# Another merge order of four walks on each engine in a twelve-block decoder

## The chip, the cores and the metric

The kernel runs on one core of a Trainium2 chip. The metric is device time in microseconds (us), from one launch of the whole program; lower is better.

## What is computed

The reference takes `x` of 8 sequences x 256 positions x 128 features, and a context of the same shape, through twelve blocks: four layers of self attention, cross attention and feed-forward. Each block adds to `x` what it computes from the layer norm of `x`:

```python
x = x + _L0_attn_ref(_layernorm(x, axis=-1), ...)     # distance scores, exp, softmax
x = x + _L0_xattn_ref(_layernorm(x, axis=-1), ctx, mask, ...)  # 16 heads, squared relu
x = x + _L0_ffn_ref(_layernorm(x, axis=-1), ...)      # three dense layers of signs
x = x + _L1_attn_ref(...)                             # 16 heads, relative bias
x = x + _L1_xattn_ref(..., ctx, ctx, mask, ...)       # 16 heads, shifted positions
x = x + _L1_ffn_ref(...)                              # 8 experts of rank 16, top 2
x = x + _L2_attn_ref(...)
x = x + _L2_xattn_ref(ctx, ctx, ..., mask, ...)
x = x + _L2_ffn_ref(...)                              # 8 experts, routed
x = x + _L3_attn_ref(...)                             # rotary, window, grouped heads
x = x + _L3_xattn_ref(..., ctx, ctx, mask, ...)
x = x + _L3_ffn_ref(...)                              # 8 experts, top 2
```

A block of one sequence needs the former block of that sequence only, except for the routed experts of L2_ffn and L3_ffn, which gather rows of several sequences.

## The kernel before

The eight sequences are split over two streams: stream 0 takes sequences 0, 2, 4, 6 and stream 1 takes 1, 3, 5, 7, and each has four PSUM banks and its own tiles in SBUF. In each block a stream works through its four sequences (items), one behind the other. All of `x` stays in SBUF.

Every one of the five engines (tensor, scalar, vector, gpsimd, sync for the DMA issues) has a program made of Python generators, which are run once, when the kernel is built; what they emit is a straight line of instructions. The generator of a block, such as `L1_ffn(s, b, j)`, yields between small pieces of work; a piece, here called a step, is some one to eight instructions, mostly with one wait for a semaphore ahead of them. `alternate` strings the blocks together into walks. An engine has four: walks 0 and 1 are the main work of stream 0 and of stream 1, walks 2 and 3 are what is done ahead for the next block's items (the norm, the q, k and v products, masks, routing) of stream 0 and of stream 1. Between the walks of one engine, and between the engines, semaphores keep data dependences; nothing else ties one walk to another.

The order in which an engine interleaves its four walks is written out in the table `TURNS`, one string for each engine. Turn `i` of the string belongs to walk `i % 4`, and its character, a digit in base 36, says how many steps that walk advances before the next turn. In "2003", walk 0 does two steps, then walk 3 does three. Each engine executes its instructions in the order emitted. `Hand.wait_ge` drops a wait whose value the engine has already waited for.

The stages stand one behind the other, with the fronts of the next block mixed in: roughly, in the time before, L0_attn to 100 us, L0_xattn to 209, L0_ffn and L1_attn to 680, L1_xattn (whose scores are shifted through DRAM, tiles `skew`, `skew_room`) to 995, L1_ffn to 1152, L2_attn and L2_xattn to 1500, L2_ffn with its sorted experts to 1675, L3_attn to 1833, L3_xattn to 1937, and L3_ffn with sorted experts to the end. In the sorted experts, rows are gathered by indirect DMAs into blocks of one expert (`sorted`), pass the two products of that expert, whose weights SyncE loads for each block (`P<-in_L3f_rows`, `kz<-in_L3f_rows`), and are written back by GpSimd's indirect DMAs (`back<-mask,block_to`), from where SyncE reads them for each item (`kz<-back`). `stacks` is room in DRAM through which pieces of q and k are moved between partitions.

Lines that the trace names most: L746 is the helper of all matmuls, L1512 of ScalarE's activations, L1838 to L1849 of VectorE's operations, L2504 GpSimd's power of a norm, L2583 its indirect write, L2680 SyncE's `dma`. L358 is `Hand.wait_ge`.

Of the kernel before, what the change touches and what calls it, by code (L numbers as in the profile page):

```python
# [52 lines left out]
    "tensor": ("0100110012003211110011001300130021002100210021002100110011001300140062002100210022001500210031002100120021001200"  # L53
        "2300120040010011001001020010101100100201001101003100110010010010220011003100110011001100111011001100210033002200"
        "1100210011001300110011003100420041001110010021100200110020010100101011001100120020101300100112001001010021002101"
        "0200110012002300110012001100410010100100202011001100321021002300110021001001410030011001010011001001010011001200"
        "1200210041003100220012001100410012001100110021003100120034002100130011001100110041001100130014001100330013001300"
        "2100110021001200110033001200110011003100110012002100210011001100120021005400110011002100120023001200210021002100"
        "1200230012001200210031001100110011001200260031001200230041001200130011001200110011004200440032001200130011001100"
        "3200210012002100120022003100120023006100120024001100110011001200230041001200240011002200310012002200220032001200"  # L60
        "1400210031001100230023003200330032001100510012001200120011001100110012001100120043002300110011002200310011001100"
        "3300110022001200130011001100310011001100120021001200220031001200110012006100120024001200210012002300410012002400"
        "1100120011004200230010100120020101030010610021002300120011004300110041003200120021001100210011002100220012002100"
        "2300110022001200110011003100110011001100210012001100211010100100211011002100110020102200120020011100100101021100"
        "1400110023002100410012001100120011001200210022002100130012001200110021001100210031002100210011001100210011001100"
        "1100210012003200210022001100220011001100120011002100120021001210010010100110120011001100111001001300130012003101"
        "1100100112020300430021001100130011002100310011002100110011002100120011002400140012002100120011002100210021002200"
        "3100410012001200110021002100130011001100210011001300110011001100110021001010212012002010020021001100120011001100"
        "1100210013002200110210010200220101001100110011001100410031001100110021001100120011001100120012001200110012002100"
        "2300210022001100110041001100410011002100110021001100110021001100110011001200230022001100110011001200110012001200"  # L70
        "1100120011001100310023003100230011001100130022001200110031003200120012002100110011002200110022001100210022001300"
        "1100310031001200120013001100120021001100220012001100110011001200230021001100310022001100210012001100140041002200"
        "3100110011001200240011002200310011003100120012001200110021002100210021001100110011001300140011002100220021001210"
        "011001001410041002100210010021002100110020013001400161007002a301010011001200210012001200110023002300130011002100"
        "1100110021001200230021001100110011001200110011001100110011001100110011101100211001001200130012004100101001002100"
        "1100110015002700110021001100110101001200210012001100220021001100200111001200500132001100140011001300110011002100"
        "1100120032001100110011100100301011003300220011001010220023001100120023002601030112001100110011003200110021001001"
        "3200120041008200110014001200110013004200210011001300210011001010210030101100111011001100110011001110210011002500"
        "1100130013010201110112003101310011002100130032001300320021006100120014001100120013004100110013001100110011001100"
        "1100220011001010202001001100110021101200110013001200110021001100230014002100110011001100210013001200210012001001"  # L80
        "1100220010011001300102002100130043001300110012001100410011001100210011001100210011001100110031001100110031001010"
        "0100201010101100130022001510410022003200110022001101220011001100220011002200110010011100110010011100100112001200"
        "1200210032002100110011001100120011003100111021001100320010104100231011001100111001002100210021001200120012002100"
        "1200110021001100300102001100220011002100110011001200130012012001110021002100400111001100120012101210010012001100"
        "1310010031001100110021001100110032001200120012102110010011001100220022001010020031001101010011011100210011001001"
        "21002100110032002300202003002100101001001101120111010a100110051008011301040103003200j001610020016001910011001100"
        "41001200220011001100210011002300210041001200420018001600151004101e100f100110c1006100101041002002a00100104010p010"
        "01010201030013001200150012001500160100104100201031005100210021009100301103010500230013001c0014016100410041004100"
        "5001200141001100140011001200110013001300110011001100110112001300240012002100110012001100230033001e00150012001100"
        "2100101002001010010022100200120010200100111021003100110021101010021010100210021005001100310011004100110011010101"  # L90
        "2200100101003200210010012001030010013200310021001100100111001001410020018100200120013001510061002200110013001b00"
        "110017001a0016001x"),
    "scalar": ("0200110010111100210014002200210011004200220011001100210012001100330011002100110022001200310022001200110011001200"
        "1001001220110011002100100100110101001001110021001101201021001100120011001100100112100100501001003100101014001300"
        "2100210011004600110011001100110032001100110011002010510020011200110011002110521001001200110011001200210010101001"
        "0010330011001601110203002100120013001200210010102200110010104010410011003010410030100100110010013100510102001400"
        "1100100101001100200102001100210023010100120011004100110011002200130021006100110031002100110031002100110011001200"
        "2100330013001200120012002100120011001500260021002200210021001300310012001100110011001100230011002200110011002300"
        "1200210011003400120011001100120012002100120012003200120022001200110011002300120011002100220012001100220012003200"
        "1200110031001100120022002200230011003200110011003200110011001100120031001100120022001100120011001100220012003100"  # L100
        "1100120011002200210011001200120031001300410012001100230021001100220011001100110012001100110022001200420011001200"
        "2200220023001100320011001100320023002200210011002200120011002200110011002300110011001010010100100101001150103010"
        "1100130012010100100101003200210011001100410011003200120011001200210011001200110012003200110023005200110021003100"
        "1200220010100100110011001010140020100100140010011001100100102300101001001200510020010100110101002100110011002300"
        "2200240021002200210031002100310011001100220011001100110011001100110021002200110022001100120021001200120042001110"
        "0110251002001200130011001200120111011100101011102001020011001100210011003001010011002100110121001100120014001100"
        "1100210021002100110012001200220021002100110031001200220021001100110011001100140031003200120011004110130011200100"
# [2892 lines left out]
```

## Time and profile before

| | us |
|---|---|
| median of three runs | 2091.87 |
| lowest and highest run | 2087.24, 2092.49 |
| the profiled execution, its own time | 2096.31 |
| its span, first to last instruction | 2094.5 |
| TensorE busy | 1745.7 |
| VectorE busy | 1438.9 |
| ScalarE busy | 1035.9 |
| GpSimd busy | 461.7 |

The profiled execution is one of its own, beside the three runs. Its span leaves out 1.8 us around the first and the last instruction. The mean clock that TensorE was granted is 0.925 of full speed. Busy time of TensorE is that of its matmuls; its weight loads run beside them. Idle time before an instruction is listed with what released it.

### The profile page before, as it was taken

To read this page: it belongs to the slowest core of one execution; us is meant where nothing else is said; L and a number is where in the kernel's file an instruction comes from. 1 tells how busy PE (TensorE), PEld (TensorE's weight loads), DVE (VectorE), ACT (ScalarE), POOL (GpSimd) and SP (SyncE) were. 2 spreads that over 40 slices of the span, in tenths; PEclk is the share of its full clock that TensorE was granted. 3 is DMA by queue.
4 is the path that set the end of the run, shared out by engine and by line. 5 is a ranking of instruction groups with operands and counts; after the bars stand their busy time and mean duration, and the time that the engine had idled before them with its cause. 6 is when DMAs were issued, how large, how long until landed. Compare 5 with 4: busy or idle time off the path is not lost.

```text
span 2094.5 us, 39958 instructions
## 1 busy us (share of the span) xinstructions
PE 1745.7 (83%) x14536; PEld 1356.6 (65%) x14536; DVE 1438.9 (69%) x4894; ACT 1035.9 (49%) x2588; POOL 461.7 (22%) x448
## 2 busy tenths in 40 slices
PE   6588999999998677779998798899878867766885
PEld 5455687776776455546887576667658855654785
DVE  6689524777877579779888677767864456567643
ACT  3277525666765556656333354455434335631342
POOL 3300110000002000000546200000464544213442
PEclk9899999999999789989999899999989879976888
DMA  5334067000001988885201323323126543332356
GB/s 179 79 74 117 16 240 231 1 1 1 1 1 37 269 214 238 245 225 152 81 1 28 90 72 89 89 59 88 48 77 190 161 120 93 77 139 84 103 153 199
DMA packets 211051, 228.56 MB, mean 109 GB/s; under 512 B 16052, under 2 KB 179276, under 8 KB 210216
## 3 DMA queue, kind: packets, MB, share of 16 engines
q1 hardware_dynamic: 205864, 215.71, 36.3%
q0 software_dynamic: 4992, 10.30, 1.4%
q8 instruction: 116, 1.90, 0.4%
q14 instruction: 79, 0.65, 0.1%
HBM read 130.57 MB, written 94.98 MB: 108 GB/s over the span
## 4 chain that ended last, share of the span: by engine, by line
PE 49%; DVE 22%; DMA 11%; ACT 7%; issue 6%; POOL 2%; SPq 2%; another core or an unknown queue 0%; DVEq 0%; ACTq 0%; POOLq 0%
PE banks L746 42%; ACT P L1512 4%; PE banks L1061 3%; DMA stacks<-region 3%; SPq L2680 2%; DVE region L1918 2%; DMA back<-mask,block_to 2%; DVE P L1838 2%; DVE negm L1849 2%; DVE P L2090 1%; ACT region L1512 1%; DVE route L1838 1%; DVE region L2160 1%; DVE region L1838 1%; PE banks L1153 1%
## 5 line engine op out<-in xcount | busy, mean ns | idle before, releaser
L2504 POOL TENSOR_TENSOR norms<-norms,consts 128x2 f32<-128x2 f32 x112 | 81.6, 730 | 1224.2 <-DVE norms L1842 1223.8
L1512 ACT ACTIVATE P<-P,negm 128x256 f32<-128x256 f32 x512 | 240.8, 498 | 114.0 <-DVE negm L2110 64.7
L1512 ACT ACTIVATE P<-banks 128x512 f32<-128x512 f32 (+2 forms) x392 | 188.4, 511 | 164.9 <-PE banks L746 155.6
L1849 DVE TENSOR_REDUCE negm<-banks 128x2 f32<-128x512 f32 (+1 forms) x264 | 149.2, 591 | 34.9 <-PE banks L746 31.1
L1512 ACT ACTIVATE region<-banks 128x384 f32<-128x384 f32 (+4 forms) x221 | 108.5, 506 | 78.1 <-PE banks L746 55.4
L746 PE MATMUL banks<-kz,qs 128*128 128x256 bf16 (+1 forms) x512 | 122.5, 275 | 27.2 <-DMA kz<-stacks 9.9
L746 PE MATMUL banks<-bands,identb 128*128 128x160 bf16 (+1 forms) x768 | 142.4, 247 | 0.0
L746 PE MATMUL banks<-xnT,region 128*128 128x256 f32 x544 | 138.8, 389 | 3.2 <-ACT xnT L1512 3.1
L746 PE MATMUL banks<-region 64*128 64x256 f32 (+6 forms) x922 | 124.6, 356 | 9.9 <-ACT region L1512 4.1
L746 PE MATMUL banks<-qv,region 128*128 128x256 bf16 (+2 forms) x512 | 114.9, 266 | 18.6 <-ACT P L1512 15.4
L746 PE MATMUL banks<-qs,kz 128*128 128x256 bf16 (+2 forms) x512 | 112.1, 262 | 17.7 <-ACT P L1512 8.9
L746 PE MATMUL banks<-kz,region 128*128 128x256 f32 x512 | 121.9, 384 | 4.0 <-DVE skew_room L1838 2.8
L2583 POOL DMA_INDIRECT back<-mask,block_to x92 | 89.4, 972 | 120.7 <-DVE mask L2338 110.1
L746 PEld LDWEIGHTS banks<-xnT,region 128*128 128x128 f32 x544 | 99.4, 194 | 21.4 <-ACT xnT L1512 6.9
L746 PEld LDWEIGHTS banks<-kz,region 128*128 128x128 f32 x512 | 95.6, 191 | 19.9 <-DVE skew_room L1838 5.1
L1838 DVE TENSOR_TENSOR P<-P 128x512 f32<-128x512 f32 (+1 forms) x136 | 84.6, 663 | 30.2 <-ACT P L1512 29.2
L746 PEld LDWEIGHTS banks<-region 128*128 128x128 f32 (+3 forms) x922 | 79.9, 160 | 36.8 <-issue 14.9
L746 PE MATMUL banks<-P,region 128*32 128x256 f32 (+6 forms) x1408 | 93.3, 325 | 10.4 <-ACT P L1512 3.7
L2110 DVE CUSTOM_DVE_ANT_0 P<-banks,region 128x256 f32<-128x256 f32 x256 | 92.7, 420 | 9.4 <-PE banks L746 9.2
L746 PE MATMUL banks<-region,identb 128*128 128x256 bf16 x384 | 98.2, 284 | 0.0
L746 PE MATMUL banks<-region,qv 128*128 128x256 bf16 (+2 forms) x384 | 79.2, 269 | 22.6 <-DMA qv<-stacks 9.6
L1153 PE MATMUL banks<-perm,P 128*128 128x128 f32 x512 | 82.2, 290 | 18.6 <-ACT P L1512 9.2
(288 smaller groups left out, 4485.2 us busy)
## 6 DMA issues: line engine op xcount, KB each, us to landing
stacks<-region SPq DMA_DIRECT2D x178, 192.0 KB, 3.0
sorted<-qs SPq DMA_DIRECT2D x4, 4160.0 KB
skew<-region SPq DMA_DIRECT2D x64, 256.0 KB
qs<-stacks SPq DMA_DIRECT2D x24, 384.0 KB
kz<-stacks SPq DMA_DIRECT2D x48, 192.0 KB
skew<-region SPq DMA_DIRECT2D x64, 128.0 KB
skew_room<-skew SPq DMA_DIRECT2D x32, 256.0 KB
P<-skew SPq DMA_DIRECT2D x32, 256.0 KB
```

Source lines behind the costliest of these rows:

```text
L746: return p.e.matmul(o, lhsT, rhs, start=start, stop=stop)
L1061: i = p.e.transpose(s.T[:, k * S + t * 128:k * S + (t + 1) * 128], s.P[:, n // 2 % 2, n % 2, t, k * 128:(k + 1) * 128], ident)
L1153: m = p.e.transpose(s.T[:, k * S + t * 128:k * S + (t + 1) * 128], s.P[:, i % 2, 0, t, k * 128:(k + 1) * 128], ident)
L1512: return a.e.activation(o, i, f, **kw)
L1838: return v.e.tensor_tensor(o, a, b, op)
L1849: return v.e.tensor_reduce(o, a, AX, op, negate=negate)
L1918: step(v.e.tensor_copy(dst, t.unsqueeze(1).to_broadcast([128, dst.shape[1], S])))
L2090: m = v.e.tensor_tensor_reduce(Pq[:, t, :], bank[:, t * S:(t + 1) * S], addend(t), -1.0, 3.0e38, ALU.add, ALU.min, s.negm[:, t, i:i + 1])
L2110: m = v.e.tensor_tensor_reduce(Pq[:, t, :], s.bank[par][:, t * S:(t + 1) * S], rel[:, h, 128 - 128 * t:128 - 128 * t + S], -1.0, 3.0e38, A ...
L2504: g.e.tensor_tensor(room[:, :, 0], room[:, :, 0], pows[:, :], ALU.pow).then_inc(done, 1)
L2583: g.e.indirect_dma_start(s.back[:, :], to, s.block_y[:, n % 2, :], None).then_inc(s.stored[n % 2], 16)
L2680: d.e.dma_start(dst, src).then_inc(sem, 16)
```

## The change

All five strings of `TURNS` are replaced, nothing else. The order in which each engine merges its four walks differs in small places all along the kernel. It was found by a local search that starts from the former order. The strings are shorter (tensor 4386 to 3262 characters, scalar 3486 to 2230, vector 4070 to 2806, gpsimd 518 to 422, sync 1074 to 642), partly as fewer turns of zero steps stand between others. The steps they count are 3686 before and 3682 after for tensor, 3151 and 3147 for scalar, 3093 for vector, 412 and 406 for gpsimd, 865 for sync; what is missing are last steps behind which a walk had nothing left to do.

The core of the diff, the beginnings of the shorter two strings:

```diff
--- before.py
+++ after.py
@@ -50,130 +50,92 @@
 TURNS = {
...
-    "gpsimd": ("1100171001001001200120101001001160101001001100120021002100110011a01020101010021004010610010400110011001100110012"
-        "0021001100220010101070011101001001001210030011002100300111001001001002001010030011002100210010012101001001001400"
-        "1100210021003001012011002200110010102100130203010310010101110011001100110011004100210012002100120022300160013001"
...
-    "sync": ("2201020014001110101010014001201020011001201040101001100200320021001100220031001100210011002200340010040103110201"
-        "0010021210100100101021002011001012001001100101001001010010010010110030101101020011003300110021002100130031001200"
-        "1200210023001100110020100100111010104100120101010101021001101430100111003002001110013001110045002100320011002100"
...
+    "gpsimd": ("50022020101200110910100100120021002100116011103001010024001001010011801040010b1200110021001100220010101080020110"
+        "1510010012005001110010010010020011100200110021002100200111101001040012001100310031010010011003100403001080010011"
+        "0011001100110011004008010021001200210012002250014001200131002100320031001410010011100210030074100313002200220012"
...
+    "sync": ("3020200231010010080010020022e01100210011001100220011003100430022002401110020080200221010030050010030400325001011"
+        "0100230055015500201033003200230032100320200102010301101060310010500327002101010055005410530102003300220033002210"
+        "3010051035010312603100105004090042010300201034005500530022001200230050100300322008010010900200305001070040020201"
...
```

## Rows read from the trace of the kernel before

**Rows 1.** The page's part 1: the span, busy time of each engine, instructions.
```profile
span 2094.5 us, 39958 instructions
...
PE 1745.7 (83%) x14536; PEld 1356.6 (65%) x14536; DVE 1438.9 (69%) x4894; ACT 1035.9 (49%) x2588; POOL 461.7 (22%) x448
```

**Rows 2.** The page's part 4: the chain's time by engine.
```profile
PE 49%; DVE 22%; DMA 11%; ACT 7%; issue 6%; POOL 2%; SPq 2%; another core or an unknown queue 0%; DVEq 0%; ACTq 0%; POOLq 0%
```

**Rows 3.** Windows: length, busy PE, PEld, DVE, ACT, POOL; granted clock, DMA share, GB/s.
```profile
0.00:209.00 209.00, 154.14 (x1216) 112.63 (x1216) 160.48 (x385) 109.57 (x203) 42.97 (x47) 0.93 0.40 112
209.00:680.00 471.00, 448.92 (x3043) 336.69 (x3042) 309.85 (x1152) 272.27 (x765) 30.67 (x33) 0.99 0.18 59
680.00:733.00 53.00, 31.63 (x247) 21.08 (x248) 29.09 (x112) 28.95 (x68) 1.36 (x2) 0.72 0.93 270
733.00:995.00 262.00, 210.73 (x1769) 149.28 (x1768) 212.66 (x745) 166.44 (x386) 10.86 (x15) 0.92 0.78 215
995.00:1152.00 157.00, 145.99 (x785) 125.64 (x784) 134.25 (x395) 52.02 (x117) 91.06 (x116) 0.98 0.11 37
1152.00:1833.00 681.00, 568.55 (x6110) 448.98 (x6109) 446.35 (x1460) 324.30 (x779) 192.99 (x137) 0.93 0.36 96
1833.00:1937.00 104.00, 66.76 (x471) 50.51 (x468) 71.56 (x310) 25.80 (x76) 28.98 (x34) 0.69 0.33 112
1937.00:2095.00 158.00, 119.01 (x910) 111.76 (x908) 74.71 (x341) 56.57 (x200) 62.81 (x66) 0.86 0.50 151
```

**Rows 4.** Timeline from 697 us: start, length, instruction, [idle before it].
```profile
699.74 0.89 SPq L2680 DMA_DIRECT2D skew_room<-skew  x2
700.68 0.98 SPq L2680 DMA_DIRECT2D P<-skew  x2
...
703.34 0.40 PE L746 MATMUL banks<-kz,qs 128*128 128x256 bf16 x1 [9.30 <-DMA kz<-stacks]
...
703.53 0.42 PE L746 MATMUL banks<-region,identb 128*128 128x256 bf16 x1
```

**Rows 5.** Timeline of PE at 710 us.
```profile
710.61 0.27 PE L746 MATMUL banks<-region,identb 128*128 128x256 bf16 x1
```

**Rows 6.** Timeline of PE, the first and last of the 100 steps.
```profile
106.41 1.92 PE L746 MATMUL banks<-xnT,region 128*128 128x256 f32 x4
...
2035.84 1.06 PE L746 MATMUL banks<-kz,OTp 128*128 128x128 f32 x8
2036.73 0.50 PE L746 MATMUL banks<-region,OTp 128*128 128x128 f32 x3
```

**Rows 7.** Timeline of PE in L2_ffn.
```profile
1623.67 1.06 PE L746 MATMUL banks<-region,P 128*128 128x128 f32 x8
...
1625.56 1.14 PE L746 MATMUL banks<-region 128*128 128x128 f32 x8
...
1627.88 1.06 PE L746 MATMUL banks<-region,OTp 128*128 128x128 f32 x8
```

**Rows 8.** Timeline of DVE in L1_ffn.
```profile
1020.03 1.41 DVE L1846 SCALAR_TENSOR_TENSOR kz<-banks,OTp 128x256 f32<-128x256 f32 x4
...
1022.07 0.42 DVE L1838 TENSOR_TENSOR P<-skew_room 128x256 f32<-128x256 f32 x1
```

**Rows 9.** Timeline of POOL, DVE and PE from 1986 us.
```profile
1987.96 0.96 POOL L2583 DMA_INDIRECT back<-mask,block_to  x1 [0.30 <-issue]
1988.95 0.72 POOL L2504 TENSOR_TENSOR norms<-norms,consts 128x2 f32<-128x2 f32 x1
1989.70 0.17 DVE L1890 COPY kz<-region 128x2 f32<-128x2 f32 x1 [2.90 <-issue]
...
1990.44 0.69 PE L1298 MATMUL banks<-perm,kz 128*128 128x128 f32 x2 [1.17 <-issue]
```

**Rows 10.** The chain at the end: start, length, what; the first and last landing.
```profile
2046.00 7.26 DMA back<-mask,block_to
...
2084.29 4.21 DMA kz<-back
```

More of the change, by code:

```diff
@@ L52 @@
 TURNS = {
[L53 to L92, printed above, removed]
@@ new lines @@
+    "scalar": ("0300320013004210230020013100110013003200230041001400420023003100140042002001001200110201004101003001100103003101"
+        "2010350053010210301060102900520055001500310043008310310023016110021032002500301020113500260010030500360040103300"
+        "3200701001100100501060100300200182010100150102003001030042003001060053005500320061005300730014007500250026004500"
+        "2500250041004300540012002200340022002200340022004600220022002400220012003200120022001200220012002300320021001300"
+        "3400110032001200120053002200120033001100320022003200130032002100110022003200130022002200120011003100230021001100"
+        "1100230012003100130041001300330032002200110012002200110011002200120042002300220022002300210022002200320023002200"
+        "2100110024001100320011001100230011001110010300205100101020102502020062001300410042003100140033001300420033001400"
+        "7100430011001300310010102300211024100400200220100300300100100200420030012201220043001400330012003200520043004300"
+        "1100340074004400440023003100132029002500231101002001202002003400400102003001220020011300490042004400440041004400"
+        "4300210024004400330011005300301014200100240022002200240101002201301002004010520122002200300103013400430014004200"
+        "4500720054004600450051003400120025002100240049003200840012002200430054002700210014001100120022003100530022003600"
+        "2100120011001100110063002300330011003200110012001200761004006010010032200110011007310013100121013200310020016001"
+        "2001b001810022001200310023005c1017001710061003001010301081001300500104002100210011006200200150013100220013010200"
+        "11002501020062001100160012001210031009003021001029004101b10080010200200181002200130105003b0027100300861003003021"
+        "001028014100a0020100310062002001a300150014003b008500110011100820030010205200310013005400200102006101510131002300"
+        "500103001501020035001800291003009010e020020029003010a00181011001020021001601040028119g00101001102100120030100100"
+        "301024005600j001610105100101030057010200110046011c00111023009201g1002100170080103001060011100e001f01060080019300"
+        "2100110011001100381001001210050021300320d1002100g00260303020010090028001l00101001101061005003010020010101m002011"
+        "3010a30160013200d1010101021001003a001010030010100m00f00230018001320182003d00220023001100150020010300180203009x00"
+        "660020100700202002006010220020300a1066010200100112001001260010010200120010014001320142011100150012001h"),
```

138 lines of the change are left out of this document (60 added, 78 removed).

## The prediction

> **What bounds the kernel now.** I read the page first. TensorE (PE) is busy for 1745.7 of 2094.5 us, the next engine, VectorE (DVE), for 1438.9 [rows 1]. That leaves PE 2094.5 - 1745.7 = 348.8 us without work, one sixth (16.7%) of the span. The chain that ended last lies on PE for 49% of the span, on DVE for 22%, on DMA for 11% and on ACT for 7% [rows 2]: PE sets the pace for long stretches, and between them the chain hops over DVE, ACT and transfers.
>
> Where these stretches lie is in the windows [rows 3]. From 209 to 680 us PE is busy for 448.92 of 471 us: no order of the work can gain much there. From 680 to 733 us it is busy for only 31.63 of 53, with the DMA engines at 93%; from 733 to 995 us for 210.73 of 262; from 1152 to 1833 us for 568.55 of 681; in the last 262 us for 66.76 + 119.01 = 185.77. An order can gain in these. It can lose most easily where two engines are full at once: from 995 to 1152 us (L1_ffn) PE has 145.99 and DVE 134.25 of 157 us.
>
> The last column but two is the granted clock of PE. It is 0.72, 0.69 and 0.86 in the stretches where PE waits most. The same product of 128x256 bf16 takes 0.42 us at 703.53, right after 9.30 us of idleness, and 0.27 us at 710.61 [rows 4, 5]; the former is at 1.2 GHz, the latter at 2.4 GHz. PE busy time times (1 - clock), summed over the eight stretches, is 10.8 + 4.5 + 8.9 + 16.9 + 2.9 + 39.8 + 20.7 + 16.7 = about 121 us: what the low clock costs today.
>
> **The change, part by part.** Only strings of digits differ. Every instruction, tile, transfer and semaphore stays, and so does the order inside each of the four walks of an engine; what differs is which walk goes first where two meet. I laid the old order and the new one over the timeline, step by step (a step is what a generator does between two yields), and for each step took its start and the moment its last input was there.
>
> Of the 2746 steps with work on PE, 452 change places; on ACT 385 of 1771, on DVE 452 of 1989, on POOL 61 of 330, on SP 134 of 493. None goes further than some 15 places. Counted in pairs, 288, 248, 335, 34 and 96 pairs of steps change sides, 1001 in all. The strings also lose a few last turns that no walk needed; they issue nothing, so they cost nothing.
>
> What can be gained: a step on the chain that stood ready behind others, and now goes ahead of them, starts earlier by at most the smaller of its own slack and the work it passes. On PE that is 46.1 us in 100 steps, of which the first is one of the two that share the row at 106.41 and the last that at 2036.73, ahead of the one at 2035.84 [rows 6]. On DVE it is 26.6 us in 43 steps, on ACT 5.7 in 14, on SP 4.6 in 6, on POOL 0.9 in 1: together 83.9 us. Three places as samples:
> - On PE an expert product of stream 1 at 1627.88 goes ahead of three steps of stream 0 that began at 1624.6: 2.06 us earlier [rows 7].
> - On DVE the softmax multiply at 1022.07, whose inputs were there at 1018.6, goes ahead of the four scaled sums of 1.41 us at 1020.03 and what follows them: 2.04 us [rows 8].
> - On POOL the norm at 1988.95, ready at 1986.4, goes ahead of the indirect write at 1987.96. DVE stood idle for 2.90 us until 1989.70 and PE for 1.17 us until 1990.44 behind it [rows 9]; about 1 us of this should really vanish.
>
> What can be lost the same way: on PE 58 of the 227 steps that are moved ahead had inputs which, at the times of before, came too late for the new place. At most they add 24.4 us of waiting. The largest is the expert product of stream 1 at 1625.56 (ready at 1625.49), put ahead of three steps from 1623.67 on, 1.82 us [rows 7]. And a step of the chain that is passed by others starts later by what passes it, so long as nothing fills that again; the bound of this is 71.7 us on PE, 63.8 on DVE, 11.6 on ACT, 13.9 on SP and 0.7 on POOL, 161.7 in all.
>
> On SP the same. Just before PE's 9.30 us of idleness, stream 1's `skew_room<-skew` (0.89 us at 699.74, ready since 672.8) goes behind stream 0's `P<-skew` (700.68) and the `skew<-region` after it: 0.99 and 1.5 us for stream 0 against 3.8 us for stream 1, which had slack [rows 4]. At the end, stream 1's weight loads go ahead of stream 0's reads of `back`, and stream 0's last store goes behind stream 1's. At most 1.3 us, since the four waits for a landing that make most of the chain there, the first 7.26 us long and the last 4.21 [rows 10], are of transfers whose order in their own stream does not change.
>
> Two large moves that I cost at nothing: the `ctxT` load at 196.7 us goes behind steps that wait until 341 us, but PE reads it only at 666.5 us; three weight loads of L3_ffn at 1921.8 us go 8 us later, for products in the 1990s. Without that cover they would cost 8 us and more.
>
> **The sum.** An earlier step shortens the kernel only where the work that it releases is what PE lacks. Between nothing and all of the 83.9 us I take PE's idle share as the price, one sixth: -14.0 us. The PE waits by the same share: 24.4 x 0.167 = +4.1. The passed steps I take at nothing, since in each exchange the one that passes does work that had to be done anyway and the idle time after it takes up the delay. Net -9.9 us. Against the profiled execution's own time, 2096.31 us, that is 2086.4. This execution lies 4.4 us above the median of the three runs (2091.87), so the forecast is 2082. Bounds: -83.9 if all of it counts, and +24.4 if nothing comes earlier and every wait on PE does.
>
> **A rule against the rows.** The rows at 703.53 and 710.61 show PE at half its clock behind an idle stretch [rows 4, 5]. The Trainium skill says, under TensorE: Matmul & The Clock Gate (Part 1, the HAM clock gate), that the default state is throttled and activity releases it: the trace agrees with that. It adds that for modelling "the ramp penalty is <1% of a typical kernel span". By that, less than 21 us would hang on the clock here, and the third rival below would be worth 2 us at most; the rows give 121 us, and I go by the rows.
>
> **Rivals.**
> - *Exchanges between equals* (2092). Two streams do the same on other batches: what one gains at a place the other loses. For it: the passed steps' 161.7 us stand against the 83.9; 471 us are full of PE work. Against it: the places where PE idles are unevenly spread, and most of the large moves let a step with waiting readers pass one with slack, like those in [rows 8, 9].
> - *DVE waits in order* (2103). This is the slower one. DVE takes 278 steps ahead of others, of which 181 had inputs that came too late for their new places; the bound of the waits is 102.8 us, of which 27.9 lie from 840 to 1260 us, around the stretch where DVE is busy for 134.25 of 157 us [rows 3]. Behind a waiting DVE instruction stand all four walks, and PE's evictions among them. If a fifth of that bound arrives, it is 20.6 us: 2096.3 - 14.0 + 4.1 + 20.6 - 4.4 = 2102.6. It turns the sign once more than a tenth (9.9 of 102.8) arrives. Against it: inputs come earlier too, as their makers were moved as well.
> - *The clock follows* (2070). If PE's idle stretches shrink, some of the 121 us of low clock goes too. A tenth of it on top of the forecast gives 2082 - 12. For it: clock and idleness go together in [rows 3]. Against it: moves of 1 to 2 us hardly break up a stretch of 9.30 us.
> - That the strings do nothing is excluded: 1001 pairs stand the other way.
>
> **How the numbers follow.** A change of 0.3% (6.3 us) is about what a measurement of this kernel can tell from no change. Forecast, -10 us with its own range of 2074 to 2086: 0.44. The clock follows: 0.11. Exchanges between equals, 2086 to 2098: 0.24. DVE waits, above 2098: 0.21. Faster is 0.44 + 0.11 = 0.55, same 0.24, slower 0.21. The range goes from 2064, past the clock's 2070 by half of what it adds, to 2104, just above the DVE rival; a tenth is left out on each side.
>
> **What the profile after would show.** Busy times of all engines the same to within a few us, except that PE's may fall with its clock. If I am right, PE's idle time falls from 349 to about 339 us, its idle 9.30 us before 703.34 becomes some 1 to 2 us shorter, the 1.17 us at 1990.44 vanish, and the windows from 733 to 995 and from 1152 to 1833 us give most of it, while 209 to 680 us keeps its length. If the DVE rival holds, DVE's idle time behind PE and ACT grows and the window of L1_ffn gets longer. If the clock follows, the windows now at 0.69 to 0.92 show higher ones. I am wrong if the exchanges that pay lie where PE has enough to do, or if a moved SP or POOL step holds back a transfer of some microseconds that no other work covers.

## The result, and the profile after

The kernel became slower: 2111.20 us median of six runs (2108.26 to 2116.21) against 2091.43 (2087.24 to 2092.97) for the kernel before on the same chip, a ratio of 1.0097 with a 95% interval of 1.0081 to 1.0113. That is about 20 us where 10 us less were forecast. The profiled execution took 2114.68 us, its span is 2112.9. Line numbers after the change are 38 lower: L708 is the former L746.

The page of the kernel after: the span, the engines' busy time, the chain by engine, which answer to [rows 1, 2].

```profile
span 2112.9 us, 39940 instructions
...
PE 1757.5 (83%) x14536; PEld 1359.6 (64%) x14536; DVE 1441.4 (68%) x4894; ACT 1035.8 (49%) x2588; POOL 460.2 (22%) x448
...
PE 50%; DVE 23%; DMA 10%; ACT 7%; issue 4%; POOL 3%; SPq 2%; another core or an unknown queue 1%; DVEq 0%; POOLq 0%; ACTq 0%
```

PE's time without work rose from 348.8 to 2112.9 - 1757.5 = 355.4 us, and its busy time by 11.8 us: nearly two thirds of the loss in the traces is PE being busy longer with the same work. The other engines are as busy as before, to within 2.5 us.

The windows of the kernel after, same columns as [rows 3], with edges set to the same steps of PE, to the nearest microsecond or two:

```profile
0.00:210.00 210.00, 155.40 (x1212) 113.11 (x1213) 160.62 (x384) 108.37 (x202) 42.94 (x47) 0.93 0.39 111
210.00:683.00 473.00, 449.99 (x3047) 336.89 (x3044) 309.49 (x1153) 273.24 (x766) 30.15 (x33) 0.99 0.18 59
683.00:735.00 52.00, 30.42 (x246) 20.60 (x247) 28.67 (x110) 29.01 (x68) 1.36 (x2) 0.72 0.96 275
735.00:1000.00 265.00, 213.96 (x1769) 151.68 (x1768) 214.06 (x747) 165.53 (x384) 10.51 (x15) 0.92 0.77 213
1000.00:1164.00 164.00, 147.31 (x786) 125.57 (x785) 138.27 (x397) 52.37 (x117) 89.91 (x117) 0.99 0.10 34
1164.00:1857.00 693.00, 579.98 (x6085) 455.21 (x6088) 443.90 (x1460) 324.30 (x777) 193.91 (x137) 0.91 0.35 95
1857.00:1959.00 102.00, 66.47 (x501) 51.26 (x495) 71.48 (x310) 26.72 (x78) 29.68 (x35) 0.72 0.32 109
1959.00:2113.00 154.00, 113.96 (x906) 105.30 (x905) 74.92 (x340) 56.25 (x199) 61.73 (x66) 0.91 0.52 159
```

L1_ffn, which was 157 us long, is 164: there PE's idle time grew by 5.7 us and its busy time by 1.3. The row from 1164 us on is 12 us longer, and here PE's busy time grew by 11.4 us, at a granted clock of 0.91 instead of 0.93. In the last row it fell by 5.1 us, at 0.91 instead of 0.86. Apart from these two rows, L1_ffn and that from 1164 us on, the lengths differ by 1 to 4 us.

The two traces hold the same steps in each walk, so each step has a start in both. How far apart the starts of the PE steps lie, and how this distance changes from one place to the next, says where time is lost. "Old" is the range of the same number, also against the trace before, in the 9 to 16 traces of experiments that had the old order in the stretch. Steps near an edge can stand in another order after the change, which makes such a number uncertain by some tenths, and at 1833 us by more than 1 us:

```
stretch of before    after - before   old order, other traces
   0 to   20 us          +1.25          -0.29 to +1.30
  20 to   46             -4.26          -1.69 to  0.00
  46 to   75             +4.69          -0.00 to +0.01
  75 to  209             -0.25          -2.35 to +0.07
 209 to  680             +1.54          -0.23 to +0.02
 680 to  995             +2.30          -2.12 to +5.95
 995 to 1150             +7.07          -0.60 to +0.24
1150 to 1500             +2.88          -0.71 to +4.11
1500 to 1675             +3.90          -6.27 to +0.86
1675 to 1790             +1.06          -3.73 to +1.42
1790 to 1833             +3.72          -0.53 to +0.93
1833 to 1937             -2.26          -0.47 to +2.23
1937 to the end          -3.27         -14.64 to -1.96
```

The column sums to +18.4 us, the difference of the spans. Some stretches with few transfers repeat to hundredths or tenths of a microsecond, those with many do not. What stands clear of the repeats is L1_ffn (+7.07), a pair in L0_attn that nearly cancels (-4.26, +4.69), L3_attn's end (+3.72), L2_ffn (+3.90 from 1500 to 1675 us) and L0_ffn with L1_attn (+1.54); clear on the other side is only L3_xattn (-2.26). L2_ffn has less behind it than its range says: of the two other traces with the new order there, e15 shows +2.1 and e3 -6.0 us.

The experiments ran on four chips in turn, and the last stretch goes by the chip: -13.8 to -14.6 us in e1 to e3, -6.7 to -9.0 in e5 to e8, -11.5 to -14.4 in e9 to e12, -2.0 to -4.4 in e13, e14 and e16 to e18, all with the old order there. So its wide range is mostly that of chips.

Two places where PE is busy longer, in the trace before and in the trace after (L2_ffn and L3_attn's end):

```profile
1500.00:1675.00 175.00, 142.55 (x1164) 121.20 (x1162) 97.58 (x450) 70.03 (x209) 100.10 (x82) 0.89 0.42 131
...
1790.00:1833.00 43.00, 34.20 (x460) 25.94 (x459) 24.96 (x92) 23.81 (x58) 9.64 (x6) 1.00 0.31 75
```

```profile
1515.00:1694.00 179.00, 147.15 (x1166) 125.52 (x1165) 97.19 (x450) 69.90 (x210) 99.79 (x82) 0.85 0.41 128
...
1810.00:1857.00 47.00, 36.45 (x436) 26.59 (x440) 25.35 (x95) 23.88 (x56) 9.83 (x6) 0.93 0.28 69
```

PE's busy time grew by 4.6 and 2.3 us in them and the clock fell from 0.89 to 0.85 and from 1.00 to 0.93. One trace of each kernel can't say whether the new order brings that about or where the low stretches happened to fall.

### The profile page after: what moved, and what is told of

Its sections match the earlier page's. It is cut to its first block, busy times and chain, and to the rows that moved or that the text cites. A ratio compares the mean times of both kernels' runs of the same rounds, so it can differ in the third digit from the quotient of the medians.

```text
span 2112.9 us, 39940 instructions
## 1 busy us (share of the span) xinstructions
PE 1757.5 (83%) x14536; PEld 1359.6 (64%) x14536; DVE 1441.4 (68%) x4894; ACT 1035.8 (49%) x2588; POOL 460.2 (22%) x448
## 4 chain that ended last, share of the span: by engine, by line
PE 50%; DVE 23%; DMA 10%; ACT 7%; issue 4%; POOL 3%; SPq 2%; another core or an unknown queue 1%; DVEq 0%; POOLq 0%; ACTq 0%
PE banks L708 43%; ACT P L1474 3%; PE banks L1023 3%; SPq L2642 2%; DVE P L1800 2%; DVE region L1880 2%; DMA skew<-region 2%; DVE negm L1811 2%; DMA stacks<-region 2%; DVE route L1800 1%; DVE skew_room L1800 1%; ACT region L1474 1%; DVE region L1800 1%; PE banks L874 1%; DMA back<-mask,block_to 1%
## 5 line engine op out<-in xcount | busy, mean ns | idle before, releaser
L708 PE MATMUL banks<-bands,identb 128*128 128x160 bf16 (+1 forms) x768 | 145.1, 249 | 0.0
L708 PE MATMUL banks<-kz,qs 128*128 128x256 bf16 (+1 forms) x512 | 121.8, 274 | 26.2 <-DMA kz<-stacks 11.1
L708 PE MATMUL banks<-xnT,region 128*128 128x256 f32 x544 | 139.9, 390 | 3.3 <-ACT xnT L1474 3.1
L708 PE MATMUL banks<-region 64*128 64x256 f32 (+6 forms) x922 | 125.3, 358 | 8.8 <-ACT region L1474 3.6
L708 PE MATMUL banks<-qv,region 128*128 128x256 bf16 (+2 forms) x512 | 116.4, 268 | 16.9 <-ACT P L1474 13.6
L708 PE MATMUL banks<-qs,kz 128*128 128x256 bf16 (+2 forms) x512 | 113.3, 265 | 18.2 <-ACT P L1474 9.6
L708 PE MATMUL banks<-kz,region 128*128 128x256 f32 x512 | 122.0, 385 | 7.2 <-DVE skew_room L1800 5.0
L708 PEld LDWEIGHTS banks<-xnT,region 128*128 128x128 f32 x544 | 99.0, 193 | 22.6 <-ACT xnT L1474 7.5
L708 PEld LDWEIGHTS banks<-kz,region 128*128 128x128 f32 x512 | 95.8, 191 | 24.9 <-DVE skew_room L1800 8.3
L708 PE MATMUL banks<-P,region 128*32 128x256 f32 (+6 forms) x1408 | 93.9, 331 | 11.9 <-ACT P L1474 6.7
L708 PEld LDWEIGHTS banks<-region 128*128 128x128 f32 (+3 forms) x922 | 80.4, 161 | 34.6 <-issue 13.7
L708 PE MATMUL banks<-region,qv 128*128 128x256 bf16 (+2 forms) x384 | 79.2, 266 | 24.7 <-ACT region L1474 11.7
L708 PE MATMUL banks<-region,identb 128*128 128x256 bf16 x384 | 98.3, 284 | 0.0
```

Of the source, the lines that this page charges most:

```text
L708: return p.e.matmul(o, lhsT, rhs, start=start, stop=stop)
```

## The experiments

All use the kernel before and change only strings of `TURNS`. The kernel before ran at 2075 to 2094 us beside them, by chip; ratios are to the runs on the same chip, and single traces are compared by stretches.

**One part of the kernel at a time.** A cut at a time t gives each walk the steps that began before t in the trace before.

```diff
-TURNS = old order
+TURNS = old order before t1, new order from t1 to t2, old order from t2 on
+# t1, t2 in us: e1 0, 995; e2 995, 1152; e3 1152, 1675; e4 1675, end
```

> The new order on all engines for the steps that began before 995 us in the old trace, the old order behind. Theory 1 (the loss is local: each stage loses by its own exchanges, and what it loses stays lost): the two traces of whole kernels stand 5.3 us apart at 995 us, so +5 us against before (2096). Theory 2 (the loss lies in one place, L1_ffn, where VectorE waits in order): within 2 us of before. Theory 3 (the loss comes from the clock, by chance of where the low stretches fall, not from the places): any size up to 10 us, not tied to the 5.3.

> The new order only for the steps between 995 and 1152 us (L1_ffn with the fronts done beside it), the old one before and behind. Theory 1: the distance between the two traces grows there from 5.3 to 12.4 us, so +7 us (2098). Theory 2: nearly the whole loss, +15 to +20 us. Theory 3: near nothing, since TensorE has its full clock there in both traces.

> The new order only between 1152 and 1675 us (L2_attn, L2_xattn, L2_ffn). Theory 1: the distance grows there from 12.4 to about 18 us, so +5 to +6 us (2097). Theory 2: within 2 us of before. Theory 3: more, as PE busy time grows there by 5 us of the 12 in all.

> The new order only from 1675 us to the end (L3_attn, L3_xattn, L3_ffn). Theory 1: the distance is about 18 us at 1675 and 19.6 near the end, with 24 between, so +1 to +2 us (2093). Theory 2: within 2 us of before. Theory 3: any size, as the clock is lowest here.

Measured: 1.0048 (1.0030 to 1.0066), 1.0048 (1.0032 to 1.0065), 1.0018 (1.0001 to 1.0036) and 1.0022 (1.0001 to 1.0044). The four sum to 1.36% where the whole change cost 0.97%. The loss is spread, against theory 2, and adds up within the intervals, for theory 1. L1_ffn is longer by 7.35 us in e2's trace, as by 7.07 in the trace after, at a granted clock of 0.98 before and 0.99 after ([rows 3] and the windows above); a loss there has nothing to do with the clock, against theory 3. Both e1 and e2 lost more in the medians than expected: 10 us where it was 5, and 11.5 where it was 7; e2's interval holds the 7, that of e1 (6.2 to 13.7 us) begins above its 5.

**L1_ffn by engine.** The new order between 995 and 1152 us on some engines alone.

```diff
-TURNS[engine] = old order
+TURNS[engine] = old order, new between 995 and 1152 us
+# engines: e5 vector; e6 tensor; e7 tensor, vector; e8 vector, scalar, gpsimd
```

> In L1_ffn (995 to 1152 us) VectorE alone in the new order, the other engines in the old one. Measured is the stretch between the PE steps that stood at 995 and at 1150 us, which was 7.1 and 7.4 us longer in the two traces with the new order on all engines, and changed by -0.6 to +0.2 us in those with the old one. Theory 1 (VectorE's order makes PE wait): +5 us or more. Theory 2 (PE's own order, steps put ahead of what feeds them): below +1.5 us. Theory 3 (only both together): below +1.5 us.

> In L1_ffn TensorE alone in the new order. Theory 1: below +1.5 us in the stretch. Theory 2: +5 us or more. Theory 3: below +1.5 us.

> In L1_ffn TensorE and VectorE in the new order, ScalarE and GpSimd in the old one. All three theories: about +7 us in the stretch; less than +5 us would say that ScalarE or GpSimd has a part.

> In L1_ffn VectorE, ScalarE and GpSimd in the new order, TensorE in the old one. Theory 1: +5 us or more, as with VectorE alone. Theory 2 and theory 3: below +1.5 us.

The stretch grew by 6.65, 3.48, 6.95 and 9.32 us. VectorE's order alone is enough for nearly the whole loss (theory 1). That TensorE's alone costs 3.48 none of the theories had; the two do not add, since 6.95 us is what both together cost, and e8, with VectorE's, ScalarE's and GpSimd's order new and TensorE's old, loses more than the whole change. Where PE then waits with VectorE's new order alone, by the waits of e5 in that stretch (total, times, longest; lines of that kernel are one lower):

```profile
PE banks L745 <- DVE pick_w L1837: 2.8, 3, 1.3
PE banks L745 <- DVE kz L1845: 2.5, 1, 2.5
...
PE banks L745 <- DVE skew_room L1837: 2.2, 3, 1.9
```

In the trace before, PE waited there once for `pick_w`, 0.6 us, never for VectorE's `kz`, and 2.8 us for `skew_room`. What is new is the waiting for the first two.

**Which of VectorE's 56 exchanged pairs.** First the 10 in which a routing step is passed: the copy of the router's logits (`route`) or the weights `pick_w`. e11 takes them out of e5, e12 has them alone. Then, alone, the 10 between steps of the two main walks that are no routing steps (e13), and the 36 in which a front's walk has a part (e14).

```diff
-TURNS["vector"] = old order
+TURNS["vector"] = old order, but of the 56 pairs that change sides in L1_ffn:
+# e11 all but the 10 with route or pick_w passed (45 of the other 46)
+# e12 these 10;  e13 10 between the main walks;  e14 36 with a front's step
```

> In L1_ffn VectorE in the new order, but the 10 of its 56 exchanges in which a routing step (the copy of the router's logits or the weights pick_w) is passed by another are undone; the other engines in the old order. VectorE's whole new order cost 6.65 us in the stretch from 995 to 1150 us. Theory 1 (the routing chain is what PE waits for): below +2.5 us. Theory 2 (the products of stream against stream and the norms of the fronts cost it): above +4.5 us.

> In L1_ffn the old order, with only those 10 exchanges on VectorE made. Theory 1: above +4 us in the stretch. Theory 2: below +2.5 us.

> In L1_ffn the old order, with only the 10 exchanges on VectorE made in which steps of the two streams' main walks pass each other (products of the gates, skew_room and P; no routing step). Theory 2a (these cost it): above +2.5 us in the stretch from 995 to 1150 us. Theory 2b (the fronts' walks cost it): below +1 us.

> In L1_ffn the old order, with only the 36 exchanges on VectorE made in which one of the two steps belongs to a front's walk (the norms and the scaled rows for the next block). Theory 2a: below +1 us. Theory 2b: above +2.5 us.

The stretch grew by 4.20, 1.49, 2.78 and -0.38 us. The routing pairs hold 1.5 to 2.5 of the 6.65 us: theory 1 fails in both runs, theory 2 holds in e12 and misses in e11 (4.20 where it said above 4.5). The 36 pairs of the fronts cost nothing alone. e13 is above the mark of theory 2a, but, as shown below, some 1.1 of its 2.78 us come from an exchange that the new order doesn't make; without it e13 lies between 2a and 2b. 1.49 + 2.78 - 0.38 = 3.9, so 2.8 us arise only when they come together.

Three places show how. In the first, VectorE before made `pick_w` first, and then a norm and a product `P` of the other stream:

```profile
1017.56 0.16 DVE L1842 TENSOR_SCALAR pick_w<-small 128x2 f32<-128x2 f32 x1
...
1018.41 0.35 DVE L1838 TENSOR_TENSOR norms<-norms 128x2 f32<-128x2 f32 x2
...
1018.87 0.42 DVE L1838 TENSOR_TENSOR P<-skew_room 128x256 f32<-128x256 f32 x1
```

After, the product and the norm go first, and `pick_w` comes last:

```profile
1024.07 0.41 DVE L1800 TENSOR_TENSOR P<-skew_room 128x256 f32<-128x256 f32 x1
1024.40 1.38 DVE L1800 TENSOR_TENSOR norms<-norms 128x2 f32<-128x2 f32 x2
...
1025.90 0.16 DVE L1804 TENSOR_SCALAR pick_w<-small 128x2 f32<-128x2 f32 x1
```

The norm's two small operations take 1.38 us between them, where they took 0.35. Each of them ends some 0.02 us after an operation that GpSimd does at the same time:

```profile
1024.24 0.84 POOL L2514 TENSOR_TENSOR kz<-P 128x256 f32<-128x256 f32 x1
1025.05 0.72 POOL L2510 TENSOR_TENSOR P<-P,OT 128x256 f32<-128x256 f32 x1
```

So about 1 us of the delay of `pick_w` is not the work that goes ahead of it but what GpSimd adds to that work. PE, which had no pause there before, stands idle for 1.17 us:

```profile
1024.21 1.13 PE L708 MATMUL banks<-kz,region 128*128 128x256 f32 x4 [0.18 <-DVE skew_room L1800]
1026.51 1.16 PE L708 MATMUL banks<-perm,pick_w 128*128 128x128 f32 x8 [1.17 <-DVE pick_w L1800]
```

The second is a sample that the prediction gave for a gain [rows 8]. The product `P` at 1022.07 and the step behind it go ahead of the four scaled sums `kz<-banks,OTp` of 1.41 us, which stood at 1020.03. In e13, VectorE's timeline is now

```profile
1019.27 0.16 DVE L1838 TENSOR_TENSOR norms<-norms 128x2 f32<-128x2 f32 x1 [0.68 <-POOL norms L2504]
1019.47 0.60 DVE L1843 TENSOR_SCALAR xn<-x,norms 128x128 f32<-128x128 f32 x2
1019.98 0.42 DVE L1838 TENSOR_TENSOR P<-skew_room 128x256 f32<-128x256 f32 x1
1020.50 0.69 DVE L1838 TENSOR_TENSOR skew_room<-banks,region 128x512 f32<-128x512 f32 x1
1021.11 1.41 DVE L1846 SCALAR_TENSOR_TENSOR kz<-banks,OTp 128x256 f32<-128x256 f32 x4
```

and PE's, which had run on without a pause,

```profile
1018.02 1.89 PE L746 MATMUL banks<-xnT,region 128*128 128x256 f32 x8
1021.91 1.35 PE L746 MATMUL banks<-kz,region 128*128 128x256 f32 x5 [2.00 <-DVE kz L1846]
```

PE waits 2.00 us, and it waits for the scaled sums. They read a PSUM bank, and PE's next product of that stream needs the bank empty. The step that was passed was the one that PE wanted; it was in time in the trace before. But not all of this belongs to the change: in e13 a front's norm and scaled rows (`norms`, `xn`) stand ahead of the sums too, with VectorE's wait of 0.68 us for GpSimd, and in the new order they do not (nor in the old). In e11, where the sums come before that norm, the pause at the same product is 0.88 us, and the distance jumps there by 1.15 us instead of 2.25. In e5 and in the trace after there is no such pause at all: PE comes there later, having stood for `pick_w`.

The third place is the largest jump of e5 in the stretch, 2.73 us at the step that stood at 1131.01. Before, VectorE made the scaled rows at 1126.19 (0.59 us), the scaled sums `kz<-banks,OTp` at 1128.38 and the residual sum `x<-x,banks` at 1129.71. In e5 the residual sum and the rows go ahead of the scaled sums. VectorE, then GpSimd, then PE:

```profile
1135.59 0.49 DVE L1837 TENSOR_TENSOR x<-x,banks 128x128 f32<-128x128 f32 x2 [1.24 <-PE banks L745]
1135.99 2.17 DVE L1842 TENSOR_SCALAR xn<-x,norms 128x128 f32<-128x128 f32 x2
1138.08 1.40 DVE L1845 SCALAR_TENSOR_TENSOR kz<-banks,OTp 128x256 f32<-128x256 f32 x4
```

```profile
1136.14 3.77 POOL L2601 CAST kz<-perm 128x2048 bf16<-128x2048 f32 x2 [3.62 <-DVE x L1837]
```

```profile
1138.88 1.13 PE L745 MATMUL banks<-kz,region 128*128 128x256 f32 x4 [2.46 <-DVE kz L1845]
```

The scaled sums stand behind a step that waits 1.24 us for PE, and behind the rows, which take 2.17 us instead of 0.59: the residual sum releases GpSimd's casts, and the rows last until the first of them has ended. The experiments take this apart. In e12 and e14 the sums still go first, and the distance doesn't jump. In e13 only the residual sum goes ahead, PE waits 0.38 us and the jump is 0.64. In e5 and e11 the rows do too, PE waits 2.46 us and the jump is 2.73 and 2.76. So 2.1 us that no part has by itself arise here. In the trace after, with TensorE's order new as well, this pause is 1.29 us.

**One step of GpSimd.** The pair at 20 to 75 us came from one step, a memset of 128x4096 bf16. In the trace before it ran at 32.98 for 3.51 us, and VectorE's `tensor_scalar` of 128x256 f32 from SBUF to SBUF, otherwise 0.28 us, lasted until it ended:

```profile
33.63 3.01 DVE L1842 TENSOR_SCALAR kz<-kz 128x256 f32<-128x256 f32 x1
```

After the change the memset runs at 48.98, and now the next item's `tensor_scalar` takes 3.49 us, with PE behind it:

```profile
48.98 3.52 POOL L2495 MEMSET region<- 128x4096 bf16 x1
49.15 3.49 DVE L1804 TENSOR_SCALAR kz<-kz 128x256 f32<-128x256 f32 x1
...
53.02 0.95 PE L708 MATMUL banks<-kz 128*128 128x256 f32 x2 [2.82 <-DVE kz L1808]
```

e9 has the old order with this one step in its new place, e10 with it behind the norm that stood at 39.20 in the trace before, where VectorE has nothing to do. The whole edit is one string:

```diff
-    "gpsimd": ("110017100100100120012010100100116010100100110012...
+    "gpsimd": ("110017100100100120012010100100110011001070010012...   # e9
+    "gpsimd": ("110017100100100120012010100100110010700100110012...   # e10
```

> The old order on every engine, but GpSimd's memset of 128x4096 bf16 (3.51 us at 32.98) is put where the new order has it, behind the norm at 51.35; nothing else moves. Theory A (VectorE's tensor_scalar from SBUF to SBUF can't start while GpSimd's memset runs): the one at 33.63, 3.01 us long, falls to 0.3 us, and PE steps come 3 to 4 us earlier at 50 us; in its new place, from about 48, the memset makes another one last over 2 us, and PE waits for it near 50 us, so that little or nothing is left at 75 us. Theory B (the norms that the memset was moved past are what helps and hurts): the long tensor_scalar stays with the norms, not with the memset. Either way within 2 us at 75 us.

> The old order on every engine, but the same memset behind the norm at 39.20, where VectorE then waits 5 us for PE. Theory A: no tensor_scalar over 1 us, no wait of PE at 35 and none at 50: the PE steps at 75 us come 3.5 to 4.5 us earlier, and the whole kernel is 0.2% faster. Theory B: no gain at 75 us.

e9 moved PE's steps by -4.27 us from 20 to 46 and by +4.71 us from 46 to 75, to 0.02 us what the whole change did there. The timeline of e9, GpSimd and then VectorE:

```profile
48.40 3.52 POOL L2533 MEMSET region<- 128x4096 bf16 x1
```

```profile
48.58 3.48 DVE L1842 TENSOR_SCALAR kz<-kz 128x256 f32<-128x256 f32 x1
```

e10 moved them by -4.28 and 0.00. In its timeline the memset runs from 36.85, after VectorE's `tensor_scalar`, which takes 0.28 us:

```profile
36.85 3.51 POOL L2533 MEMSET region<- 128x4096 bf16 x1
```

```profile
33.34 0.28 DVE L1842 TENSOR_SCALAR kz<-kz 128x256 f32<-128x256 f32 x1
```

Theory A holds. The whole kernel measured 0.9983 (0.9964 to 1.0002), 2076.32 us median against 2079.99: the size fits, and the interval just touches no change. The Trainium skill says this under SBUF — State Buffer (Who interferes with whom): VectorE and GpSimd share a pair of ports, an instruction such as `tensor_scalar` in a two-port mode and a GpSimd instruction can't hold it together, and the one that starts later "fully blocks". The trace agrees: 3.01 and 3.49 us for an operation of 0.28, each ending some 0.15 us after the memset.

**The clock takes part.** The stall holds PE for 2.38 us in the trace before and for 2.82 after, and the loss is 4.3 and 4.7. The windows of the kernel before (clock in the last column but two) show what comes after the stall, PE busy all the time at a mixture of 1.2 and 2.4 GHz:

```profile
33.00:37.00 4.00, 1.65 (x10) 1.30 (x10) 4.00 (x5) 1.33 (x4) 3.49 (x1) 1.00 0.88 284
37.00:41.00 4.00, 3.98 (x11) 3.21 (x12) 2.55 (x11) 0.00 (x0) 0.72 (x1) 0.59 0.97 307
```

The kernel after has the same behind its stall:

```profile
53.00:57.00 4.00, 3.98 (x11) 3.21 (x12) 2.08 (x7) 0.00 (x0) 0.00 (x0) 0.57 0.02 4
```

e10 in the whole stretch:

```profile
33.00:41.00 8.00, 7.54 (x43) 6.62 (x41) 3.98 (x18) 3.49 (x7) 4.18 (x2) 1.00 0.85 272
```

At a granted clock of 0.57 to 0.59, 4 us of PE work hold 4 x 0.41 to 4 x 0.43 = 1.6 to 1.7 us of loss, which is the rest. In e10 the clock stays at 1.00.

**Undoing the places found, and L3_xattn.** e15 is the whole new order, but with L1_ffn in the old order and the memset in its free place. e16 is the old order with the memset in its free place and the new order between 1833 and 1937 us.

```diff
-TURNS = new order
+TURNS = new order, old between 995 and 1152 us; memset behind the norm of 39.20   # e15
-TURNS = old order
+TURNS = old order, new between 1833 and 1937 us; memset behind the norm of 39.20  # e16
```

> The new order everywhere but in L1_ffn (995 to 1152 us, old), and GpSimd's memset in its free place behind the norm at 39.20. The whole new order was 20 us slower. If the losses are local and add up: 20 - 7.1 for L1_ffn - 4.7 for the memset's new place = +8 us (2088 where before has 2080). Rival (the stages lean on one another, so that a repair in one place is lost again behind it): +15 us or more.

> The old order, with GpSimd's memset in its free place and the new order on all engines between 1833 and 1937 us (L3_xattn). If that stretch gains by itself: -4.3 - 3.3 = -7.6 us (0.9963). Rival (it was only shorter as it gave back what the stretch before had lost): the memset's -4.3 us alone (0.998) or less.

e15 measured 1.0032 (1.0012 to 1.0053), or +6.7 us; the two repairs bring back 0.65 points of the 0.97, as the sum of places said. One of them is more than a repair: the memset's free place is worth 4.3 us that the kernel before doesn't have either, so what the other places lose together is 6.7 + 4.3 = 11 us. e16 measured 0.9980 (0.9962 to 0.9997), 2089.39 against 2092.72: faster than the kernel before by 3.3 us, about the memset's part. Nothing of L3_xattn's shorter stretch can be told from the runs. In e16's trace it is 1.1 us shorter, against 2.3 in the trace after and 3.1 in e4, where the stretch before it had lost 3.7 and 5.5 us; so part of the gain there is loss given back.

**L3_attn's end.**

```diff
-TURNS[engine] = old order
+TURNS[engine] = old order, new between 1790 and 1833 us   # e17 all, e18 vector
```

> The new order on all engines between 1790 and 1833 us only. If the loss arises there: +3.5 to +5 us in the stretch from 1790 to 1833 us, where traces with the old order differ by -0.5 to +0.9 us. If it was brought along from the stretch before: below +1.5 us.

> The new order on VectorE alone between 1790 and 1833 us. If VectorE's order makes it: +3 us or more. If it is TensorE's or ScalarE's order: below +1.5 us.

The stretch grew by 2.13 us in e17 and by -0.11 in e18. So VectorE's order alone is not it. Against 3.7 us in the trace after and 5.5 in e4, e17 has 2.1; its clock stays at 1.00 in the stretch, where it is 0.93 in the trace after and 0.86 in e4. Whether the rest needs the new order before 1790 or is the clock's, and which step it is, stays open.

## Why the prediction was wrong

- **The sign.** The forecast was -9.9 us, the measured change about +20. The step that failed is in the sum: "The passed steps I take at nothing". Their bound stood there, 161.7 us, twice that of the steps that come earlier (83.9). I dropped it with the argument that the step that passes does work that had to be done anyway and the idle time after it takes up the delay. VectorE's new order in L1_ffn alone made the stretch 6.65 us longer. Its largest jump, 2.73 us, is a passed step that PE needed next, and what went ahead of it was more than work to be done anyway: a wait of 1.24 us, and an operation of 2.17 us instead of 0.59 while GpSimd's cast ran.
- **The sample on VectorE** at 1022.07 was counted as a gain of 2.04 us. In e11 and e13 it belongs to a stop of PE, 0.88 and 2.00 us, the latter with a norm ahead as well. In the trace after PE has no pause there, but nothing is gained either. The slack of the step that goes ahead was read from the trace, the slack of the one passed was not.
- **The sample on PE** at 1627.88 came where forecast in the order, but the step went ahead only together with the one at 1625.56 of [rows 7]; from 1602 to 1632 us the distance grew by 0.72 us in the trace after and fell by 0.51 in e3. No gain can be seen.
- **The sample on GpSimd** was right in mechanism and wrong in size: "about 1 us of this should really vanish". The norm does go first and VectorE's pause falls from 2.90 to 1.64 us, but PE's is 1.07 instead of 1.17 [rows 9]. GpSimd's timeline and then PE's after the change:

```profile
2008.99 0.72 POOL L2466 TENSOR_TENSOR norms<-norms,consts 128x2 f32<-128x2 f32 x1
2009.91 1.03 POOL L2545 DMA_INDIRECT back<-mask,block_to  x1 [0.20 <-issue]
```

```profile
2010.48 0.44 PE L1260 MATMUL banks<-perm,kz 128*128 128x128 f32 x2 [1.07 <-issue]
```

- **The 9.30 us** before 703.34 [rows 4] were to become 1 to 2 us shorter by SP's new order. They are 9.24:

```profile
707.21 0.40 PE L708 MATMUL banks<-kz,qs 128*128 128x256 bf16 x1 [9.24 <-DMA kz<-stacks]
```

- **The windows.** 733 to 995 and 1152 to 1833 us were to give most of a gain; they are 3 and 12 us longer. That 209 to 680 us keeps its length is right to 1.54 us.
- **The DVE rival** had the right sign, engine and stretch for the largest single part: VectorE's new order alone gives 6.65 us where the whole change gives 7.07 in L1_ffn. It had the mechanism in part. It spoke of VectorE waiting for late inputs, bound 27.9 us around that stretch, and such a wait, 1.24 us for PE, does stand ahead of the passed sums at the largest place. But with that wait alone PE lost only 0.38 us (e13). More comes from VectorE being busy with another step while PE waits, above all with one that GpSimd makes longer: the rows of 2.17 us there, the norm of 1.38 us ahead of `pick_w`. Its price, 20.6 us for the whole kernel, netted to +11 in its 2103; the loss outside L1_ffn was not shown to be VectorE's, and e18 says that at one place it is not VectorE's alone. It had 0.21 where the forecast had 0.44.
- **The exchanges between equals** would need the sum of the places to be zero. Of the places clear of the repeats, all but the first of the L0_attn pair and L3_xattn are losses.
- **The clock rival** fails as a gain: the mean granted clock is 0.925 before and after. The clock does take part, on both sides: as at 37 and 53 us, lower in L2_ffn and at L3_attn's end, higher in the last stretch.
- **The range** ended at 2104 and the median lies at 2111. The bound of PE's waits alone, +24.4, would have held it. The range was drawn to the price of one rival and left out that the passed steps' bound was the largest number of all.
- **What was not seen at all** is the memset. GpSimd's steps were costed by their own slack; that one of them makes another engine's operation ten times as long was in the trace before, in the row at 33.63. The same holds, more mildly, for the two places in L1_ffn: which VectorE operation meets a GpSimd operation is changed by an exchange, and no term of the sum had it.

Shown by experiments, then, are the 7 us of L1_ffn and the memset's pair, out of about 20. Open stays where the other 11 us come from step by step, why e1's medians stand 10 us apart where its trace shows about 5, and how much of the 11.8 us that PE is busy longer is clock and how much less overlap between its matmuls: in L2_ffn and at L3_attn's end the clock is lower, but from 1152 to 1500 us it is 0.96 in both traces and PE is still 3.4 us busier.

## What to carry to other kernels

Where one engine is busy nearly all the time, ask of every exchange on another engine not how long the step that goes ahead had stood ready, but how late the step that is passed may be: in time by the trace is not the same as with room to spare. Count for the step that goes ahead what it waits for and how long it takes in its new company, not how long it took before. A step of GpSimd has a second price, the operations of VectorE that last longer beside it, so a free memset belongs where VectorE waits for another engine. An experiment that moves only some pairs of an order can bring pairs that neither order has; read its timeline before its number. And where a trace repeats to hundredths of a microsecond, it can settle a stretch in one run that the time of the whole kernel can't settle in twelve.

## What the runs showed of the hardware

- A GpSimd memset of 3.5 us held a VectorE `tensor_scalar` of 128x256 f32 from SBUF to SBUF for its whole length: 3.01, 3.49 and 3.48 us in three traces instead of 0.28; PE then lost 4.3 to 4.7 us, of which 1.6 to 1.7 by the clock it was granted behind the pause.
- Other GpSimd operations did the same to VectorE in L1_ffn: a cast of 128x2048 from f32 to bf16 made two `tensor_scalar` of 128x128 f32 last 2.17 us instead of 0.59 (e5), and beside two of its `tensor_tensor` of 128x256 f32, two `tensor_tensor` of 128x2 of VectorE lasted 1.38 us instead of 0.35 (trace after).
- A pause of PE of 2.38 us (before) and of 2.82 us (after) was followed by about 4 us at a granted clock of 0.59 and 0.57; without the pause (e10) it was 1.00.
- The same order repeats to 0.01 us over 29 us (46 to 75) and to 0.25 over 471, also from chip to chip. From 1937 us to the end, where the chain is transfers [rows 10], the trace before and 16 others of the same order lie up to 14.6 us apart, but those of one chip at most 2.9. The kernel before had medians of 2075, 2080 and 2093 us and a single run of 2084 on four chips.
